# Cross-attention and experts on one core: maxima spread among the values products, key projections in the score banks, shift products entered first

## The reference, cut to what matters

```python
def _L0_xattn_ref(x, context, Wq, Wk, Wv, Wo, bo):   # HEADS 8, DIM_HEAD 64, INNER 512
    q = (x @ Wq).reshape(B, S, HEADS, DIM_HEAD).transpose(0, 2, 1, 3)
    k = (context @ Wk).reshape(B, L, HEADS, DIM_HEAD).transpose(0, 2, 1, 3)
    v = (context @ Wv).reshape(B, L, HEADS, DIM_HEAD).transpose(0, 2, 1, 3)
    attn = jnp.einsum('bhsd,bhld->bhsl', q, k) * scale
    attn = jax.nn.softmax(attn, axis=-1)
    out = jnp.einsum('bhsl,bhld->bhsd', attn, v)
    out = out.transpose(0, 2, 1, 3).reshape(B, S, INNER)
    return out @ Wo + bo
...
x = x + _L0_xattn_ref(_layernorm(x, axis=-1), ctx_768, L0_xattn_Wq, ...)
x = x + _L0_ffn_ref(_layernorm(x, axis=-1), L0_ffn_router_w, ...)
```

## Time and profile before

| | |
|---|---|
| runs | 464.14, 465.06, 468.87 us, median 465.06 |
| the profiled execution | 468.46 us, of which the span from the first to the last instruction is 466.6 |
| busy share of the span | PE 92%, DVE 62%, POOL 58%, ACT 50% |
| mean granted TensorE clock | 0.963 of full speed |
| chain that ended last | PE 37%, DVE 12%, ACT 4%, issue 4%, POOL 3% |

### The profile page before, as it was taken

How to read it: one execution, slowest core, us unless ns; L and a number is a source line. 1 busy time by engine, 2 the same in 40 slices (tenths; PEclk the granted TensorE clock), 3 DMA queues, 4 the chain that set the end, 5 groups by cost and what they waited for, 6 DMA issues and landing times.

```text
span 466.6 us, 9560 instructions
## 1 busy us (share of the span) xinstructions
PE 426.9 (92%) x3650; PEld 329.2 (71%) x3650; DVE 290.1 (62%) x596; ACT 235.6 (50%) x367; POOL 269.5 (58%) x183
## 2 busy tenths in 40 slices
PE   7998988898989988898899898989998987999997
PEld 6577674767577776666776776677767675687896
DVE  4737674748482676657633767677447595768653
ACT  4366163426167263524382627152736263589873
POOL 4404995486663185928360868291806569078982
PEclk8579997999899999899999999999999999999999
DMA  7400000200000002000000002000000000410500
GB/s 225 113 2 2 2 2 1 54 2 2 1 2 1 1 2 55 1 1 2 1 1 1 2 11 95 1 2 1 0 2 1 2 2 3 130 52 3 180 24 22
DMA packets 17139, 11.75 MB, mean 25 GB/s; under 512 B 10188, under 2 KB 14136, under 8 KB 17096
## 3 DMA queue, kind: packets, MB, share of 16 engines
q1 hardware_dynamic: 17096, 11.15, 8.8%
HBM read 10.55 MB, written 0.56 MB: 24 GB/s over the span
## 4 chain that ended last, share of the span: by engine, by line
PE 37%; DVE 12%; ACT 4%; issue 4%; POOL 3%; DVEq 0%; ACTq 0%; POOLq 0%
PE ps L1141 11%; DVE maxes L890 6%; PE ps L995 6%; PE ps L997 5%; PE ps L1126 5%; PE ps L996 5%; DVE rden L831 3%; PE ps L1071 3%; ACT probs L772 2%; POOL work L473 2%; DVE kq_lo L887 1%; POOL kq_lo L688 1%; PE ps L1024 1%; DVE work L835 1%; ACT kq_hi L733 1%
## 5 line engine op out<-in xcount | busy, mean ns | idle before, releaser
L772 ACT ACTIVATE probs<-ps 128x1024 f32<-128x1024 f32 (+1 forms) x112 | 105.8, 962 | 148.4 <-PE ps L1126 145.0
L890 DVE TENSOR_REDUCE maxes<-ps 128x1 f32<-128x402 f32 x256 | 130.9, 568 | 72.6 <-PE ps L1071 71.4
L473 POOL TENSOR_TENSOR work<-work,probs 128x1024 f32<-128x1024 f32 x60 | 142.8, 2381 | 4.7
L471 POOL TENSOR_TENSOR work<-probs 128x1024 f32<-128x1024 f32 x15 | 35.7, 2377 | 135.1 <-issue 97.6
L1141 PE MATMUL ps<-probs,v_sb 128*64 128x256 f32 (+1 forms) x832 | 98.3, 395 | 0.0
L1071 PE MATMUL ps<-kq_hi 64*128 64x402 f32 x256 | 79.2, 412 | 20.4 <-DVE maxes L890 15.4
L1126 PE MATMUL ps<-kq_hi 64*128 64x256 f32 (+1 forms) x416 | 91.2, 296 | 3.7 <-ACT probs L772 2.4
L1126 PE MATMUL ps<-kq_hi,kq_lo 64*128 64x256 f32 (+1 forms) x416 | 85.6, 280 | 0.0
L1126 PE MATMUL ps<-kq_lo,kq_hi 64*128 64x256 f32 (+1 forms) x416 | 85.5, 279 | 0.0
L1126 PE MATMUL ps<-shift_rows,ones_r 64*128 64x256 f32 (+1 forms) x416 | 85.3, 279 | 0.0
L1141 PEld LDWEIGHTS ps<-probs,v_sb 128*64 128x64 f32 (+1 forms) x832 | 60.5, 142 | 33.8 <-issue 7.7
(11 more groups left out here) (149 smaller groups left out, 634.8 us busy)
## 6 DMA issues: line engine op xcount, KB each, us to landing
v_sb<-weight_rows SPq DMA_DIRECT2D x12, 256.0 KB, 4.0
raw<-in_ctx_T_dram SPq DMA_DIRECT2D x3, 600.4 KB, 4.5
work<-in_L_ffn_rw_dram SPq DMA_DIRECT2D x1, 1024.0 KB, 7.0
shift_rows<-neg_row SPq DMA_DIRECT2D x64, 0.5 KB, 2.0
raw<-weight_rows SPq DMA_DIRECT2D x4, 256.0 KB, 3.6
raw<-in_ctx_T_dram SPq DMA_DIRECT2D x3, 150.8 KB, 2.4
x_sb<-in_x_dram SPq DMA_DIRECT2D x1, 384.0 KB, 5.6
wo_sb<-in_L_xattn_Wo_dram SPq DMA_DIRECT2D x1, 256.0 KB, 5.0
```

Of the source, the lines that this page charges most:

```text
L471: ops.tensor_tensor(acc, probs[:, (n - 1) % SLOTS], pr, ALU.add).then_inc(summed, 1)
L473: ops.tensor_tensor(acc, acc, pr, ALU.add).then_inc(summed, 1)
L772: nc.scalar.activation(dst, src, ACT.Exp, scale=SCALE).then_inc(probs_ready, 1)
L890: v.tensor_reduce(maxes[:, p % 2, i * T + t, blk:blk + 1], src[:, 0:BW], AX.X, ALU.max).then_inc(ring_taken, 1)
```

## The change

- In the projections of the pairs from 2 on, the keys no longer use the ring. Blocks 0 and 1 go to the two banks of the pair-before-last's sixth unit, 2 and 3 to those of its seventh, each behind a wait for that unit's exponential. The first scores of a pair then wait until the next pair's keys are taken from those banks.
- A pair's 16 maxima stand otherwise: two ahead of the values of the pair two before, four ahead of its fourth unit's values, two ahead of its sixth's, two behind the row sums, and the other six behind units 1, 3 and 4 of the scores (before: three ahead of the values, three behind, ten behind units 0 to 4). The quotients stand behind units 0 and 2.
- VectorE's last step of the adds moves from ahead of the first values product to a step `add` ahead of the sixth unit's values, behind the maxima there.
- In the scores of a full unit, the shift product is entered first, once for both chunks of a head: 512 columns, the moving operand `shift_rows` read twice over by a step of zero.
- At the start `WARM` is 21 and `REST_1` 3. GpSimd and no longer VectorE takes the low part of the first keys' weights, and the first keys wait for that alone. The rounding of the third context block and of the values' weights comes earlier, and the first chunks of the values' projection stand among the maxima of block 1 on.

```diff
@@ -19,10 +19,11 @@
 from concourse import mybir
 
 P = 128
-WARM = 18
-REST_1 = 4
+WARM = 21
+REST_1 = 3
 TOP = 2
-EARLY_MAXIMA = 3
+AMONG_VALUES = ((0, 2), (3, 4), (5, 2))
+BEHIND_VALUES = 2
 LAG = 3
 SLOTS = 7
 ALU = mybir.AluOpType
@@ -57,32 +58,34 @@
         b, p = order[n]
         return [("ring", ("k", b, p, 0)), ("ring", ("q", b, p))] + [("ring", ("k", b, p, k)) for k in range(1, blocks)]
 
+    before_scores = sum(count for _, count in AMONG_VALUES) + BEHIND_VALUES
     first, second = keys(0), keys(1)
     v0 = [("v0", c) for c in range(chunks)]
-    out = first[:2] + [("ctx0", 2)] + first[2:3] + [("ctx0", 3)] + couples[0] + couples[1] + first[3:4]
-    out += [("wv", 0)] + couples[2] + couples[3] + first[4:] + [("m", 0)]
+    out = first[:2] + [("wv", 0)] + first[2:3] + couples[0] + [("ctx0", 3)] + couples[1] + first[3:4]
+    out += v0[:1] + couples[2] + v0[1:2] + couples[3] + v0[2:3] + first[4:] + [("m", 0)]
     for i, pair_of_maxima in enumerate(couples[4:]):
-        out += pair_of_maxima + v0[i:i + 1]
+        out += pair_of_maxima + v0[3 + i:4 + i]
     out.append(("shift", order[0]))
-    rest = v0[len(couples) - 4:]
+    rest = v0[len(couples) - 1:]
     out += rest[:2]
     for i, x in enumerate(second):
         out += [x] + rest[2 + i:3 + i]
-    out += rest[2 + len(second):] + maxima[1][:2 * EARLY_MAXIMA]
+    out += rest[2 + len(second):] + maxima[1][:before_scores]
 
     for n, (b, p) in enumerate(order):
-        ahead = maxima[n + 1][2 * EARLY_MAXIMA:] if n + 1 < n_order else []
+        ahead = maxima[n + 1][before_scores:] if n + 1 < n_order else []
         behind = 2 if n == 1 else 0
         for u in range(n_units):
             out.append(("scores", (b, p, u)))
-            out += ahead[:2]
-            if ahead and len(ahead) <= 2:
-                out.append(("shift", order[n + 1]))
-            ahead = ahead[2:]
+            if n and u in (behind, behind + 2):
+                out.append(("quotient", order[n - 1] + ((u - behind) // 2,)))
+            if u in (1, 3, 4):
+                out += ahead[:2]
+                if ahead and len(ahead) <= 2:
+                    out.append(("shift", order[n + 1]))
+                ahead = ahead[2:]
             if (n, u) == (1, 1):
                 out.append(("sums", order[0]))
-            if n and u in (behind, behind + 1):
-                out.append(("quotient", order[n - 1] + (u - behind,)))
 
         vs = [("ring", ("v", b, c)) for c in range(chunks)] if p == 0 and b else []
         projections = keys(n + 2)
@@ -109,12 +112,18 @@
             out += [("w2", e) for e in range(experts)]
         out += [("w1", k) for k, at in enumerate((0, 2, 3)) if n == at]
         following = maxima[n + 2] if n + 2 < n_order else []
-        out += following[:EARLY_MAXIMA]
-        out += [("values", (b, p, u, j)) for u, unit in enumerate(key_units(chunks)) for j in range(len(unit))]
+        for u, unit in enumerate(key_units(chunks)):
+            for at, count in AMONG_VALUES:
+                if u == at:
+                    out += following[:count]
+                    following = following[count:]
+            if u == AMONG_VALUES[-1][0] and n:
+                out.append(("add", (b, p)))
+            out += [("values", (b, p, u, j)) for j in range(len(unit))]
         if b and p == 1:
             out += [("roots", b - 1), ("norm", b - 1)]
         out += [("sums", (b, p))] * (0 < n < n_order - 1)
-        out += following[EARLY_MAXIMA:2 * EARLY_MAXIMA]
+        out += following[:BEHIND_VALUES]
     return out
 
 
@@ -205,16 +214,23 @@
 
     O_BANK = 7
     kinds = [kind for kind, _ in steps]
-    ring_banks, ring_last, held = [], [], {}
+    ring_banks, ring_last, held, early_last = [], [], {}, {}
     for n, (kind, w) in enumerate(steps):
         if kind == "ring":
             k = len(ring_banks)
             lowest = 2 if n < kinds.index("scores") else 4 if n < kinds.index("first") else 5
+            if n > kinds.index("scores") and not early_last:
+                early_last.update(held)
+            if w[0] == "k" and n > kinds.index("scores"):
+                last = (w[1] * PAIRS + w[2] - 1) * NU - 1
+                ring_banks.append(2 * ((last - (w[3] < 2)) % 2) + w[3] % 2)
+                ring_last.append(None)
+                continue
             bank = min(range(lowest, O_BANK), key=lambda i: held.get(i, -1))
             ring_banks.append(bank)
             ring_last.append(held.get(bank))
             held[bank] = k
-    LAST_OF = [max((k for k, bank in enumerate(ring_banks) if bank == i), default=0) for i in range(O_BANK)]
+    LAST_OF_4 = max(k for k, bank in enumerate(ring_banks) if bank == 4)
     hi_no = {w: i for i, w in enumerate(w for w in ring_list if w[0] in ("k", "q"))}
 
     def quarter(i):
...
@@ -612,11 +628,14 @@
                 g.tensor_tensor(ctxT_lo[:, b % 2, cs], ctx_raw[:, cs], ctxT_hi[0:C, b % 2, cs].bitcast(F32),
                                 ALU.subtract).then_inc(ctx_lo_ready, 1)
 
-            for i in range(BLOCKS):
+            pool.wait_ge(w0_hi_ready, 1)
+            g.tensor_tensor(wk_lo[:, 0:P], wk_sb[:, 0:P], wk_hi[:, 0:P].bitcast(F32), ALU.subtract).then_inc(w0_ready, 1)
+            for i in range(3):
                 low_part(0, i)
             pool.wait_ge(s_wv, 16)
             pool.wait_ge(wv_hi_ready, 1)
             g.tensor_tensor(wv_lo[:], wv_sb, wv_hi[:].bitcast(F32), ALU.subtract).then_inc(w_split, 1)
+            low_part(0, 3)
             pool.wait_ge(w_rest_hi_ready, 1)
             own(g.tensor_tensor(wk_lo[:, P:INNER], wk_sb[:, P:INNER], wk_hi[:, P:INNER].bitcast(F32), ALU.subtract))
             pool.wait_ge(pool_done, done[0])
@@ -628,7 +647,7 @@
             pool.wait_ge(s_rw, 32)
             then_own(g.tensor_copy(rw_hi[:], rw_sb[:]))
             g.tensor_tensor(rw_lo[:], rw_sb[:], rw_hi[:].bitcast(F32), ALU.subtract).then_inc(w_split, 1)
-            pool.wait_ge(w0_ready, 1)
+            pool.wait_ge(wq0_ready, 1)
             pool.wait_ge(w_rest_ready, 1)
             g.memset(wrow, 0.0).then_inc(wrow_zero, 1)
             pool.wait_ge(wrow_zero, 1)
@@ -711,12 +730,13 @@
                 ins.then_inc(xn_ready, 1)
 
             act.wait_ge(s_wqk, 32)
-            nc.scalar.copy(wk_hi[:, 0:P], wk_sb[:, 0:P])
+            nc.scalar.copy(wk_hi[:, 0:P], wk_sb[:, 0:P]).then_inc(w0_hi_ready, 1)
             nc.scalar.copy(wq_hi[:, 0:P], wq_sb[:, 0:P]).then_inc(w0_hi_ready, 1)
             for i in range(2):
                 high_part(0, i)
             act.wait_ge(setup_filled, 1)
             nc.scalar.copy(xnT_hi[:, 0:S], ps[:, 7, 0:S]).then_inc(first_ready, 1)
+            high_part(0, 2)
             for kind, w in steps:
                 if kind == "m":
                     act.wait_ge(s_wqk1, 32)
@@ -854,9 +874,8 @@
                 ins = v.tensor_scalar(xn[:, t, :], x_sb[:, t, :], mv[:, t, 0:1], rstd[:, t:t + 1],
                                       ALU.subtract, ALU.mult)
             ins.then_inc(xn0_ready, 1)
-            dve.wait_ge(w0_hi_ready, 1)
-            v.tensor_tensor(wk_lo[:, 0:P], wk_sb[:, 0:P], wk_hi[:, 0:P].bitcast(F32), ALU.subtract)
-            v.tensor_tensor(wq_lo[:, 0:P], wq_sb[:, 0:P], wq_hi[:, 0:P].bitcast(F32), ALU.subtract).then_inc(w0_ready, 1)
+            dve.wait_ge(w0_hi_ready, 2)
+            v.tensor_tensor(wq_lo[:, 0:P], wq_sb[:, 0:P], wq_hi[:, 0:P].bitcast(F32), ALU.subtract).then_inc(wq0_ready, 1)
             dve.wait_ge(first_ready, 1)
             v.tensor_tensor(xnT_lo[:, 0:S], ps[:, 7, 0:S], xnT_hi[:, 0:S].bitcast(F32), ALU.subtract
                             ).then_inc(setup_taken, 1)
@@ -864,8 +883,7 @@
             for kind, w in steps:
                 if kind == "scores" and w[2] < NU - 1 and adds(w[0] * PAIRS + w[1], w[2]) == "dve":
                     add_probabilities(v, dve, then_own, w)
-                if kind == "values" and w[2:] == (0, 0) and w[:2] != (0, 0):
-
+                if kind == "add":
                     add_probabilities(v, dve, then_own, (w[0], w[1], NU - 1))
                 if kind == "quotient":
                     quotient(*w)
@@ -1047,12 +1065,17 @@
                         cols, q = slice(w[2] * P, (w[2] + 1) * P), slice(b * S, (b + 1) * S)
                         if w[2] == 0:
                             pe.wait_ge(*(taken(("xn", 1)) if b else (setup_taken, 1)))
+                        if (b, w[2]) == (0, 0):
+                            pe.wait_ge(wq0_ready, 1)
                         ins = three(dst[:, 0:S], wq_hi[:, cols], wq_lo[:, cols], xnT_hi[:, q], xnT_lo[:, q])
                     elif w[0] == "k":
                         cols, first = slice(w[2] * P, (w[2] + 1) * P), min(w[3] * BW, L - BW)
                         if (b, w[3]) == (0, 0):
                             pe.wait_ge(*((w_rest_ready, 1) if w[2] else (w0_ready, 1)))
                         pe.wait_ge(ctx_lo_ready, BLOCKS * b + w[3] + 1)
+                        pair = b * PAIRS + w[2]
```

(23 more changed lines are left out.)

## The result

The changed kernel takes 480.69 us in the median (480.11 to 482.61), against 464.6: a ratio of 1.0337, 95% interval 1.0264 to 1.0409. Forecast were 456, and faster. Ratios leave out executions in the slower of two states that the chip shows, and medians do not, so that the one can't be worked out from the other. The profiled execution took 480.71, its span is 478.9 (before 466.6).

A forecast was written before the change was run, and what follows sets the result against it. VectorE's work, in the wrong place, was taken to hold up TensorE; 468.5 - 6.4 (pairs) - 3.0 (clock) - 1.2 (start) = 457.9, less 1.7 for a median execution gave 456 us, range 444 to 466.

The forecast's parts named there:

- What bounds the kernel: In an ordinary pair of 21.3 us, VectorE's work (14.6 us) is in the wrong place, not too much.
- Scores and projections: Plain pair: scores gain 2.1, projections 1.9, 4.0 in all; the values start at 11.1, against 15.1.
- The values stage pays some of it back: Values stage: eight maxima and VectorE's add make it 9.0 long, before 6.2; a pair takes 20.1 against 21.3.
- third rival: Values stage: each maximum's product costs TensorE up to 0.44, not 0.12; 474 midway, slower; chance 0.10.
- second rival: Values stage: VectorE's add takes 2.3, not 1.4, beside GpSimd's work; row sums wait 0.9 more; 468; chance 0.12.
- -6.4: Sum over the pairs, in us: -7.2 - 1.2 + 0.2 + 1.8.
- Where it costs: Behind pairs 5 and 9: normalisation ends at 5.6, next first exponential 4.1 late; +0.2 and +1.8 for two pairs each.
- The clock, -3.0: Two of three stretches at 1.2 GHz after projections stages would go: -3.0, between 0 and -6.
- The start: Before the first scores: either the clock falls, -1.2 (taken, chance 0.44), or it holds, -9.0.
- case (b): Start: clock holds, first scores at about 28.7 instead of 36.5, -7.8 - 1.2 = -9.0; as a rival 448, chance 0.29.
- The shifts: Scores: two products of 512 columns replace four of 256 per full unit; 192 products fewer, taken as 0.
- The slower one: The third rival: turning between forms of product in the values stage costs TensorE; 474 midway; chance 0.10.

The follow-up runs named there:

- add_earlier: The changed kernel with VectorE's add ahead of the two maxima of the sixth unit's values instead of behind them: 461.61 us, ratio 0.9832.
- awake: The changed kernel with 36 small products put in while TensorE waits for the normalisation in pairs 6 and 10: 477.91 us, ratio 1.0186.
- norm_later: The changed kernel with the normalisation behind the next pair's fourth exponential instead of ahead of its first: 469.47 us, ratio 1.0069.
- start_only: The kernel before with the start of the changed one alone: 462.53 us, ratio 0.9931.
- maxima_undone: The changed kernel with maxima, quotients and VectorE add placed as before: 456.14 us, ratio 0.9732.
- undone_norm: The changed kernel with maxima, quotients and VectorE add as before, and the normalisation behind the next pair's fourth exponential: 456.44 us, ratio 0.98.
- shift_only: The kernel before with the wide shift product alone: 466.18 us, ratio 1.0031.
- add_at_three: The changed kernel with VectorE's add ahead of the four maxima of the fourth unit's values: 476.16 us, ratio 1.0213.

## Why the prediction was wrong

**What bounds the kernel: right.** VectorE's work did stand in the wrong place, and with it well spread the kernel takes 443.15, less than any sum of mine.

**Scores and projections: right.** In pair 7 the last exponential ends 8.7 behind the row sums (said 8.85) and the keys start at 8.4 (8.25), after an idle 0.52 (0.65). The maxima ahead of the values start at 11.1 (10.8) and the values at 11.5 (11.1): right in kind, 0.4 late.

**"The values stage pays some of it back": the step that failed.** From the first values product to the end of the row sums it was to take 9.0 and takes 9.6. With the 0.4 that it begins late, a pair takes 21.1 and not 20.1, of 21.3 before. The order was the one described, add behind the maxima. What was mis-sized is the way to that add: 0.15 before the keys, 0.2 in the projections and 0.1 in the first two maxima, 0.33 in the group of four (1.48, where the sum had 1.15), 0.1 in the values products and 0.1 in the row sums. The turn for the two later maxima (0.37, said 0.2) is not on that way. So the third rival's mechanism is there at about a third of its 1.3. VectorE's add itself took 1.41 (said 1.38), so the second rival's is not. Over 14 boundaries this 1.0 is 14 of the 24 us between -6.4 and +17.2.

More than the number, the judgement was off: I saw a wait of 1.35 us of TensorE on the add in my own schedule and took it as the price of spreading the maxima. `add_earlier` shows that it was the price of one place in VectorE's queue, 19 us in all. In pair 7 GpSimd was done 3.2 us before the add began, and still 0.8 us before it in `add_earlier`.

**"Where it costs", behind pairs 5 and 9: mechanism right, price short.** The first exponential came 5.4 behind the row sums (said 5.6). But the wait was priced as a delay alone. Standing still for 3.9 us, TensorE lost its clock, 2.0 of the 4.4 to 4.7 by which each of these sums fell short (`awake`). Another 2.0 is the 1.0 for each of the two pairs; 0.4 to 0.7 is left over. `norm_later` gives 11 us back.

**The clock, -3.0: not so.** Two of the three low stretches did go, but others came: it is 1.2 GHz from about 30 to 37, 67 to 74, 184 to 190, 286 to 293 and 402 to 405. Outside the old start that was 13.6 us before and is 24 now. The 10 us more cost 5 at most, where I had 3.0 gained. The 2.0 behind each of pairs 5 and 9 is part of them. I counted those that would go and none that would come.

**The start: between the two cases.** I took the clock to fall (-1.2). It held at 2.4 GHz until about 30 and fell during the ten maxima ahead of the first scores: -5.0. Two windows of the changed kernel:

```profile
28.00:30.00 2.00, 1.85 (x5) 0.80 (x5) 2.00 (x5) 0.00 (x0) 0.00 (x0) 0.98 0.01 4
30.00:32.00 2.00, 2.00 (x13) 1.73 (x15) 2.00 (x5) 0.00 (x0) 0.00 (x0) 0.50 0.00 0
```

In `start_only`, with six maxima there, it did not fall, and -7.9 in the profiled executions is near the -7.8 of case (b) for the first exponential. The traces agree: of the executions whose clock held that far, the six with ten maxima all lost it between 29.8 and 31.9, and the three with six (`start_only`, `maxima_undone`, `undone_norm`) did not. No run changes the number of these maxima alone.

**The shifts: right.** The product of 512 columns is followed after 0.23 us (281.65 to 281.88 in pair 10), as two of 256 would be, and alone it makes no gain: the interval of `shift_only` even lies just above 1.

**The rivals.** None named what came. The slower one named the turns between products, priced 474 at its middle, and was given 0.10. It was the right stage, but its price alone would not have made the kernel slower: the turns are some 0.4 of the 1.0 lost in a pair. That the late add, the normalisation behind it and the clock behind that form one chain was in no rival.

What stays open: pairs 0 and 1 lost 3.1 together. In pair 0 the low clock until 37 can account for its share: `maxima_undone`, with the full clock there, takes 18.8 between these exponentials, the changed kernel 21.8 and the kernel before 20.0. The loss in pair 1, and the 1.1 to 1.3 by which pairs 3 and 11 take longer than pair 7, were not taken apart.

## What to carry to other kernels

Where work is spread in an in-order queue, look at what stands behind it: here two maxima of 0.5 us ahead of an add delayed row sums, the next pair and a chain through a third and fourth engine. Place a step on which others wait in the gap that the queue already has, no earlier than its own input (`add_at_three`) and ahead of what nobody awaits. Size a group of products that share a ring of banks in PSUM, the memory that products write, by the number of banks in it: here three. And when a wait of several us is forecast on TensorE, price the clock behind it too.

## What was not expected of the hardware

- Dense small products during a wait of 3.94 us kept the granted clock at 1.00 where it had been 0.74 over 13 us, and gave 2.0 us back each time.
- The clock of the same program can differ from one execution to the next: with the new start it stayed at 2.4 GHz from 10 to 26 us in nine profiled executions and fell at 12.0 in the tenth, which put the first exponential at 39.02 and not near 30 to 33.
- A TensorE shown busy for 19.70 of 20 us did not regain the full clock in the kernel before: it stayed at 1.2 GHz from 8 to 28.
- Two maxima's products among values products cost TensorE 0.37 us and three 0.56, while two between scores units are followed after 0.19 to 0.33 us (pair 7).
